# An 18-slot ring for the hidden units, with weighted sums and tail one slot later

## The reference, cut to what matters

```python
hi = jnp.einsum('bsh,hk->bsk', x, W1[:H])
hj = jnp.einsum('bsh,hk->bsk', x, W1[H:])
h = jax.nn.relu(hi[:, :, None, :] + hj[:, None, :, :] + b1)   # 128 x 128 pairs per graph
y = jnp.einsum('bijk,kl->bijl', h, W2) + b2
y = _layernorm(y, gamma, beta)
out = jnp.einsum('bij,bijh->bih', adj, y)
```

## Time and profile before

| | |
|---|---|
| median of 3 runs | 2771.56 us (2769.07 to 2772.95) |
| profiled execution | 2773.57 us, of which the span of instructions is 2772.0 us |
| PE busy | 2707.0 us (98%) |
| DVE busy | 2618.7 us (94%) |
| ACT busy | 2565.2 us (93%) |
| POOL busy | 2491.0 us (90%) |
| mean granted PE clock | 0.989 |

### The profile page before, as it was taken

How to read it: one execution, slowest core, us unless ns; L and a number is a source line. 1 busy time by engine, 2 the same in 40 slices (tenths; PEclk the granted TensorE clock), 3 DMA queues, 4 the chain that set the end, 5 groups by cost and what they waited for, 6 DMA issues and landing times.

```text
span 2772.0 us, 60903 instructions
## 1 busy us (share of the span) xinstructions
PE 2707.0 (98%) x10882; PEld 1128.4 (41%) x10882; DVE 2618.7 (94%) x20102; ACT 2565.2 (93%) x6903; POOL 2491.0 (90%) x3498
## 2 busy tenths in 40 slices
PE   8999999999999999999999999999999999999993
PEld 2344444444444444444444444444444444444442
DVE  4999999999999999999999999999999999999997
ACT  7999999999999999999999999999999999999991
POOL 3899999999999999999999999999999989999992
PEclk9999999999999999999999999999999999999995
DMA  3655655655555555556556555555555565465552
GB/s 104 239 195 211 234 198 197 230 215 192 214 226 202 204 216 222 195 213 234 195 198 235 209 192 227 223 193 210 226 207 195 205 234 203 192 228 222 193 214 108
DMA packets 188668, 571.72 MB, mean 206 GB/s; under 512 B 70656, under 2 KB 106368, under 8 KB 139136
## 3 DMA queue, kind: packets, MB, share of 16 engines
q1 hardware_dynamic: 188288, 567.83, 54.5%
HBM read 555.17 MB, written 8.39 MB: 203 GB/s over the span
## 4 chain that ended last, share of the span: by engine, by line
PE 59%; DVE 13%; ACT 11%; DMA 10%; issue 5%; SPq 2%; POOL 0%; DVEq 0%; POOLq 0%; ACTq 0%
PE y_ps L416 41%; PE ss_ps L428 11%; DVE h L684 8%; ACT h L555 6%; DMA cb<-c_scratch 6%; ACT sq L565 3%; DMA c_scratch<-c 2%; DMA devs<-dev_rows 2%; SPq L324 1%; ACT dev_rows L572 1%; PE prod_bank L478 1%; PE prod_bank L482 1%; DVE h L668 1%; DVE stats L708 1%; DVE gT L684 1%
## 5 line engine op out<-in xcount | busy, mean ns | idle before, releaser
L923 POOL TENSOR_SCALAR h<-vT,uT 128x128 f32<-128x128 f32 x2520 | 2063.8, 834 | 54.1 <-ACT vT L545 44.6
L684 DVE CUSTOM_DVE_ANT_0 h<-h,cb 128x128 f32<-128x128 f32 x8192 | 2005.8, 291 | 74.4 <-DMA cb<-c_scratch 71.4
L416 PE MATMUL y_ps<-h,w2c 128*128 128x512 f32 x4096 | 2032.8, 613 | 11.9 <-DVE h L668 2.8
L555 ACT ACTIVATE h<-uv_ps,uT 128x128 f32<-128x128 f32 x4785 | 1426.9, 441 | 0.0
L565 ACT ACTIVATE sq<-y_ps,b2c_col 128x1024 f32<-128x1024 f32 x1024 | 1193.5, 1166 | 139.3 <-PE y_ps L416 138.6
L416 PEld LDWEIGHTS y_ps<-h,w2c 128*128 128x128 f32 x4096 | 672.9, 190 | 944.1 <-issue 647.3
L684 DVE DVE_READ_ACCUMULATOR2_ANT gT<- 128x1 f32 x8192 | 637.5, 78 | 0.0
L428 PE MATMUL ss_ps<-sq,sel 128*32 128x512 f32 x4096 | 545.5, 605 | 0.8 <-ACT sq L565 0.8
L914 POOL TENSOR_TENSOR rs<-var_eps,minus_half 128x1 f32<-128x1 f32 x448 | 297.9, 665 | 35.1
L911 POOL TENSOR_TENSOR var_eps<-mv,eps_col 128x1 f32<-128x1 f32 x448 | 94.8, 212 | 132.7 <-DVE mv L711 129.2
L668 DVE TENSOR_SCALAR h<-vT,uT 128x128 f32<-128x128 f32 x757 | 202.1, 295 | 4.7 <-ACT mask_all L610 2.6
(11 more groups left out here) (100 smaller groups left out, 1460.6 us busy)
## 6 DMA issues: line engine op xcount, KB each, us to landing
cb<-c_scratch SPq DMA_DIRECT2D x384, 1024.0 KB, 9.4
cb<-c_scratch SPq DMA_DIRECT2D x256, 512.0 KB, 4.9
adj_c<-in_adj_dram SPq DMA_DIRECT2D x512, 8.0 KB
devs<-dev_rows SPq DMA_DIRECT2D x512, 8.0 KB
x_in<-in_x_dram SPq DMA_DIRECT2D x64, 64.0 KB, 10.9
c_scratch<-c SPq DMA_DIRECT2D x128, 32.0 KB, 1.5
adj_in<-in_adj_dram SPq DMA_DIRECT2D x64, 64.0 KB, 4.4
x_res<-in_x_dram SPq DMA_DIRECT2D x64, 64.0 KB, 5.3
```

The source lines that it names most:

```text
L416: op = pe.matmul(y_ps[:, t % 2, c0:c0 + COLS], w2c[:], h[:, t, c0:c0 + COLS], start=True, stop=True)
L555: op = act.activation(h[:, t, n * P:(n + 1) * P], v, ACT.Relu, bias=uT[:, b, i:i + 1])
L684: op = dve.tensor_tensor_reduce(h[:, t, cols], h[:, t, cols], cb[:, t // 2, c0:c0 + P], 1.0, 0.0, ALU.mult, ALU.add, gT[:, i:i + 1])
L923: op = pool.tensor_scalar(h[:, t, n * P:(n + 1) * P], vT[:, b, :], uT[:, b, i:i + 1], 0.0, ALU.add, ALU.max)
```

## The change

The buffer of units gets 18 slots, used as a ring: a unit of running slot number 16 g + t lies in place (16 g + t) mod 18 and may be written when the sums of the unit 18 slots earlier are done. The weighted sums run one slot later (lag 19), and so does every tail step from `g_keep` on, while the steps before it (adjacency turn, row sum, degree, sum of coefficients, `x_base`) stay. `turn_x` and `keep_xT` go one slot later. `ROOTLESS` is changed; ACT's units per slot become, from s = 0: 6 4 5 1 6 4 6 4 6 4 6 4 6 5 5 5. On SP the straightening of the new graph's half 0 is issued ahead of the result store.

```diff
-TTR_LAG = START + 14
-TAIL_LAG = START + 28
+TTR_LAG = START + 15
+H_RING = 18
-ROOTLESS = (1, 2, 4, 6, 8, 10, 13, 15)
+ROOTLESS = (1, 2, 3, 5, 7, 9, 11, 14)
...
-    ("g_keep", 2, 4), ("l0_mm", 3, 0), ("l0_sum", 3, 5), ("ln0", 3, 6), ("x1_scaled", 4, 6),
-    ("l1_agg", 5, 0), ("l1_agg_keep", 5, 8), ("l1_mm", 6, 0), ("l1_bias", 6, 7), ("l1_relu", 7, 0),
+    ("g_keep", 3, 4), ("l0_mm", 4, 0), ("l0_sum", 4, 5), ("ln0", 4, 6), ("x1_scaled", 5, 6),
+    ("l1_agg", 6, 0), ("l1_agg_keep", 6, 8), ("l1_mm", 7, 0), ("l1_bias", 7, 7), ("l1_relu", 8, 0),
...
-    ("l3_agg0", 12, 4), ("l3_agg_keep0", 13, 2), ("l3_mm0", 13, 4), ("l3_sum0", 14, 2),
-    ("l3_ln0", 14, 3), ("l3_relu0", 16, 2), ("l3_agg1", 19, 0), ("l3_agg_keep1", 19, 8),
-    ("l3_mm1", 20, 0), ("l3_sum1", 21, 1), ("l3_ln1", 21, 2), ("l3_relu1", 22, 6),
+    ("l3_agg0", 13, 4), ("l3_agg_keep0", 14, 2), ("l3_mm0", 14, 4), ("l3_sum0", 15, 2),
+    ("l3_ln0", 15, 3), ("l3_relu0", 17, 2), ("l3_agg1", 20, 0), ("l3_agg_keep1", 20, 8),
+    ("l3_mm1", 21, 0), ("l3_sum1", 22, 1), ("l3_ln1", 22, 2), ("l3_relu1", 23, 6),
...
-        h = sb("h", [P, SLOTS, DUO_UNITS * P])
+        h = sb("h", [P, H_RING, DUO_UNITS * P])
...
+                if new is not None:
+                    straighten_deviations(new, 0)
                 if oldest is not None:
                     wait_apart(sp, normed["ln3"], oldest + 1)
                     wait_apart(sp, out_stored, 16 * oldest)
                     sp.dma_start(out[oldest], x4[:, 1 - buf, :]).then_inc(out_stored, 16)
                 if new is not None:
-                    straighten_deviations(new, 0)
                     store_coefficients(new, 0)
...
-                    if s == 11 and after is not None:
+                    if s == 12 and after is not None:
                         turn_x(after, 1 - buf)
...
-                    wait(act, ttr_done, SLOTS * (g - 1) + t + 1)
+                    wait(act, ttr_done, SLOTS * g + t - H_RING + 1)
...
-                op = act.activation(h[:, t, n * P:(n + 1) * P], v, ACT.Relu, bias=uT[:, b, i:i + 1])
+                op = act.activation(h[:, (SLOTS * g + t) % H_RING, n * P:(n + 1) * P], v, ACT.Relu, bias=uT[:, b, i:i + 1])
...
-                    if s == 12 and after is not None:
+                    if s == 13 and after is not None:
                         keep_xT(after, 1 - buf)
```

More of the change, by code:

```diff
@@ L415, in products @@
                 c0 = block_of_duo * COLS
-                op = pe.matmul(y_ps[:, t % 2, c0:c0 + COLS], w2c[:], h[:, t, c0:c0 + COLS], start=True, stop=True)
+                op = pe.matmul(y_ps[:, t % 2, c0:c0 + COLS], w2c[:], h[:, (SLOTS * g + t) % H_RING, c0:c0 + COLS], start=True, stop=True)
                 if block_of_duo == 1:
@@ L662, in hidden @@
                 if n == 0:
-                    wait(dve, ttr_done, SLOTS * (g - 1) + t + 1)
+                    wait(dve, ttr_done, SLOTS * g + t - H_RING + 1)
                     if t <= 1:
@@ L667, in hidden @@
                 i = unit_of(t, n)
-                op = dve.tensor_scalar(h[:, t, n * P:(n + 1) * P], vT[:, b, :], uT[:, b, i:i + 1], 0.0, ALU.add, ALU.max)
+                op = dve.tensor_scalar(h[:, (SLOTS * g + t) % H_RING, n * P:(n + 1) * P], vT[:, b, :], uT[:, b, i:i + 1], 0.0, ALU.add, ALU.max)
                 if n == vector_units(g, t) - 1:
@@ L683, in weighted_sum @@
                 c0 = (t % 2) * DUO_UNITS * P + n * P
-                op = dve.tensor_tensor_reduce(h[:, t, cols], h[:, t, cols], cb[:, t // 2, c0:c0 + P],
+                op = dve.tensor_tensor_reduce(h[:, (SLOTS * g + t) % H_RING, cols], h[:, (SLOTS * g + t) % H_RING, cols], cb[:, t // 2, c0:c0 + P],
                                               1.0, 0.0, ALU.mult, ALU.add, gT[:, i:i + 1])
@@ L917, in hidden @@
             def hidden(g, b, t, n):
-                wait(pool, ttr_done, SLOTS * (g - 1) + t + 1)
+                wait(pool, ttr_done, SLOTS * g + t - H_RING + 1)
                 if t == 0:
@@ L922, in hidden @@
                 i = unit_of(t, n)
-                op = pool.tensor_scalar(h[:, t, n * P:(n + 1) * P], vT[:, b, :], uT[:, b, i:i + 1], 0.0, ALU.add, ALU.max)
+                op = pool.tensor_scalar(h[:, (SLOTS * g + t) % H_RING, n * P:(n + 1) * P], vT[:, b, :], uT[:, b, i:i + 1], 0.0, ALU.add, ALU.max)
                 if n == DUO_UNITS - 1:
```

## The result

The changed kernel takes 2755.2 us (4 runs, 2754.79 to 2755.48) against 2771.64 us: a ratio of 0.9942, 95% interval 0.9924 to 0.9959. The forecast was 2759.5. The profiled span went from 2772.0 to 2753.5 us.

The account below looks back on a forecast made before the run. PE was taken as the bound, losing 0.51 us a graph to ACT. Regular -8, irregular -6 and end +1 gave -13: 2760.6 us profiled, 2758.6 from the median; stated 2759.5, range 2744 to 2776.

Parts of the forecast that it names:

- PE is the bound: Whole run before: PE busy 98%, losing 0.51 us of each 42.05 us graph to ACT, and nothing else regular.
- Slot 6 to 7: PE's four passes there: ACT's units come earlier, so neither wait nor late weights, gain 0.37 us a graph.
- Slot 14 to 15: Before slot 15's block 0: ACT's units come later, a new PE wait of 0.28 us a graph.
- Swap: Rival, chance 0.18: `keep_xT` holds ACT 0.32 us, wait at slot 15 is 0.44, +0.03 a graph, 2768 us.
- slower: Rival, chance 0.10: slots 13 and 14 copies hold ACT for whole durations; PE waits 0.60 at slot 15, 2780 us.
- Regular sum: Per graph -0.37 - 0.04 + 0.28 = -0.13 us, times 61 = -8 us.
- slot 1: Slot 0 to 1: units come 0.2 us earlier as `l3_relu0` leaves the place ahead; gain 0.04 us a graph.
- Irregular: Of 7.3 us taken as the price of late `cb`, the later sums take 6 away, range 3 to 7.3.
- End: End of the run, bound by DVE with one slot more to do: +0.8 us, range 0 to 2.5.
- Ring alone: Unit writers wait for sums of 18 slots earlier: one slot more slack, gain only where the ring held anyone.
- Inversion waits grow: DVE at line 692: its waits were to grow while `cb` waits go near zero; no size given.
- POOL's ninth unit: Slots 1 to 3: a ninth unit takes 0.84 us, over a microsecond before PE wants it in slot 4; costs nothing.

Follow-up runs that it names:

- E12: Tail-only with three extra 64 KB loads on SP's queue ahead of each coefficient spread, making `cb` late: 2941.46 us, ratio 1.0617.
- E3: Changed kernel with `keep_xT` one slot later, at the end of slot 14: 2745.78 us, ratio 0.9914.
- E4: Changed kernel with the copy of xT made twice in slot 13: 2766.0 us, ratio 0.9989.
- tail-only: Kernel before with the change's later tail, unit split and SP order, but 16 slots of h and lag 18: median 2758.9 us over nine runs.
- E11: Changed kernel with three extra 64 KB loads on SP's queue ahead of each coefficient spread, making `cb` late: 2761.89 us, ratio 0.9970.
- E1: First run of tail-only, against the kernel before: 2755.77 us, ratio 0.9950.
- E5: Changed kernel itself, measured again beside tail-only: 2755.47 us, ratio 0.9945.
- E6: Tail-only measured again, beside the changed kernel: 2759.28 us, ratio 0.9956.
- E2: Kernel before with the ring of 18 slots and nothing else: 2768.92 us, ratio 1.000.
- E7: Changed kernel with the old `ROOTLESS` list of slots where POOL takes three units: 2756.27 us.
- E8: Changed kernel with SP's order of before, result store ahead of the straightening: 2756.7 us, ratio 0.9948.
- E9: Changed kernel with POOL's third unit moved from slot 14 to slot 13: 2745.82 us, ratio 0.9912.

## Why the prediction was right, point by point

- *PE is the bound, and it loses 0.51 us a graph to ACT.* Right: the changes of the regular period in the twelve runs could be read as such waits of PE for ACT and their late weights, but for E12's, where DVE with its waits for `cb` became the bound. *And nothing else regular* was not complete, see the regular sum below.
- *Slot 6 to 7: -0.37.* Right: 2.26 became 1.88.
- *Slot 14 to 15: +0.28.* Right: 0.27, with the units at 5.31 us after slot 13's squares as computed, and 0.15 for the copy. E3 and E4 show that this path is the cause. The rule of the Trainium skill ("ScalarE: Activation LUTs", section "What ACT_TABLE_LOAD costs") that back-to-back activations overlap by about 93 ns would have given 0.28 with the row of 0.37 in the kernel before, and gives 0.22 with the one of 0.31 here. The trace disagrees: the row lasts 0.31 and the next starts after 0.15, an overlap of 0.16. The measurement decides. "Swap" and "slower", the rivals that hung on this price, fall with it.
- *Regular sum: -0.13; measured -0.199.* A term was left out. A product behind a bias product (of `l3_mm` or `l2_mm2`) has its second pass 0.05 late. Before, three such places stood outside the places of late weights (starts 482 to 483 ns apart where 429 is normal); now two do, as that of `l2_mm2` has come to stand ahead of the sums of squares, and slot 14's falls on a pass that is late already. In the traces the four terms are -0.376 at slot 7, -0.046 at slot 1, +0.277 at slot 15 and -0.053 here, -0.198 together. Over 60 graphs the regular term is 11.9 us, not 8, and this is some 4 of the 5.5 us by which the profiled execution (2755.1) lies below the 2760.6 of the sum.
- *Irregular: -6.* The size was right for the profiled pair (7.3 to 0.45), and this is in part luck: it was a property of one execution, not of the kernel, and in the two runs of tail-only it was 0.6 and 5.15. The reason holds: the cover by the later lag is shown by E11 and E12. Its worth in a normal run is 2 to 4 us (E1, E5 and E6).
- *End +0.8.* Right, +0.9.
- *Ring alone: nothing.* Right (E2).
- *Inversion waits grow.* Wrong: 35.6 us after 36.7. DVE's slack went to line 753.
- *POOL's ninth unit costs nothing.* Right, but the reckoning for POOL left out what the change takes away ahead of another product. Where a straightening lands late, the inversion waits, the degree comes late and POOL's root with it, and behind the root stand POOL's units. The changed kernel's timeline of such a graph, on DVE, POOL and PE:

```profile
1252.50 0.55 DVE L693 RECIPROCAL invs<-devs 128x64 f32<-128x64 f32 x1 [1.38 <-DMA devs<-dev_rows]
...
1254.80 0.55 POOL L907 TENSOR_TENSOR dis_raw<-degree_floor,minus_half 128x1 f32<-128x1 f32 x1 [2.10 <-DVE degree_floor L733]
1255.34 4.98 POOL L924 TENSOR_SCALAR h<-vT,uT 128x128 f32<-128x128 f32 x6
...
1259.95 0.39 PE L403 MATMUL uv_ps<-xT,w1b 128*128 128x128 f32 x2
1260.46 1.10 PE L417 MATMUL y_ps<-h,w2c 128*128 128x512 f32 x2
```

  From 1259.95 to 1260.46 is 0.51 where 0.22 is regular. The product at 1260.46 is block 1 of slot 3, which needs the units made for slot 2. The last of these is the sixth behind the root, not the ninth: it ends at 1260.32. Both lists put three units in slots 1 and 2, and E7, which has the old list, shows the wait too. In all 16 such graphs of seven profiles (the changed kernel, E4, E5, E7, E8, E9, E11) PE starts 0.15 us behind the end of the sixth. What has changed is PE's way there. In the kernel before:

```profile
1394.52 0.39 PE L402 MATMUL uv_ps<-xT,w1b 128*128 128x128 f32 x2
...
1395.41 1.02 PE L416 MATMUL y_ps<-h,w2c 128*128 128x512 f32 x2
```

  There `l0_mm` and a product of the other tail stood in between, 0.67 us that have moved to slot 4, and roots that ended 4.52 us ahead of `make_uv` (5.5 is regular) held nobody up; in E9 one of 4.58 costs 0.09. No run moved these products alone. This one graph is 0.36 of the 0.45 us that are irregular in the changed kernel's profile.

## What to carry to other kernels

In a pipeline written out by hand, find which start-to-start distances of the bounding engine differ from those of the same instruction elsewhere: most excesses are late producers, others belong to what stands ahead (the 0.05 behind a bias product), and their sum is what rescheduling can win while that engine stays the bound. For each moved step, count what lies between the producer's last forced start and the instruction waited for, and also which wait the step used to hide where it stood. When the producer has no pause for several slots, take work off before that stretch or push it past its end; moved about inside, it comes back as the next wait. Slack against a slow transfer shows little in a good run and much when the transfer is late: test it by making the transfer late.

## What the runs showed of the hardware

A 128 x 128 copy of ACT from PSUM holds it for 0.15 to 0.17 us although its row lasts 0.31 to 0.37. A PE product whose operands come just in time pays 0.10 us more, on its second pass, where its weights were not loaded ahead (0.53 between starts in place of 0.43), and 0.04 where they began 0.06 ahead. The store of 32 KB of coefficients in DRAM lands in 1.5 us in the median, but in the kernel before 10 of 128 took over 2.5 and the longest 3.7, and how often differs between executions of one kernel: the runs of the kernel before spread over 5.5 us on one chip and those of tail-only (E1) over 5.1, while the changed kernel's stayed under 2. And on ACT the durations printed grow when it has no pause (squares from 1.11 at 1411.53 to 1.28 at 1419.06 in the changed kernel), while the starts keep their distance. In E7 the growth was real delay for PE: 0.62 from the start of the fourth unit in place of 0.52.
